# Info and mask spread over the partitions by DMA instead of by matmuls, in a fused convolution, attention and expert kernel

## The chip, the cores and the metric

The kernel runs on one core of a Trainium2 chip (trn2). The metric is the device time of one execution in microseconds, the median of several runs. A core has five engines that run side by side, each through one fixed list of instructions: TensorE (PE) for matmuls, VectorE (DVE), ScalarE (ACT), GpSimd (POOL), and SyncE (SP), which here issues all DMA transfers. They wait for each other through semaphores.

## The reference

The input `x` is 32 images of 64 channels and 32 x 32 pixels. Three layers follow each other, each added to its input:

```python
# layer 1, on the group-normalised input (32 groups of two channels)
info = relu(info_w @ x + info_b)          # 16 rows
mask = sigmoid(mask_w @ x + mask_b)       # 16 rows
expanded = mask[:, :, None] * info[:, None, :]    # 256 rows: each mask row times each info row
x = x + relu(out_w @ expanded + out_b)
# layer 2: linear attention of 8 heads on the layer-normalised tokens, with a two-layer MLP
t = t + attention(layernorm(t))
# layer 3: 8 experts, each W2 @ gelu(W1 @ t + b1) + b2, weighted by the two largest gates
t = t + experts(layernorm(t))
```

What the change touches is `expanded`: each of 16 info rows and 16 mask rows has to stand on the 128 partitions in copies, so that VectorE can multiply them.

## The kernel before

Two images lie on the 128 partitions as a pair, and two pairs ("slots" s = 0 and 1) make a group; there are eight groups. A group goes through some 70 named stages (the *dense* part: statistics, group norm, info and mask, products, `conv_out`, four layer norms, attention, MLP), then the *router* (`gates` to `weights_1`), then 32 expert *units* (expert e, slot s, half c of 512 pixels).

The work of several groups is interleaved. A *turn* runs the dense stages of group a, the router of group a-1 and units of the groups a-1 and a-2. `SCHEDULE` lists the stages of a turn in order; beside each name stand the steps of units that follow it on PE ("H" is a first layer, "Y" a second layer), and how many GELUs on ACT and combines on DVE follow it there. The units before the entry `first_unit` are the last of the older group. All engines run the same list, each with its own part of a stage. Groups 0 and 1 (`EARLY`) are done in an opening of their own (`OPENING`, names with `next` are group 1's), with no units beside them; group 1 uses other buffers there (`convolution_buffers`). Turns 2 to 7 are the full ones.

Info and mask (`info_mask`): PE computes both into PSUM for a slot, 32 rows for each half of the pixels in four strips of 32 partitions; ACT applies ReLU or tanh; DVE splits the result into two float32r parts (`IM`). Six *replicates* a slot (`replicate`, the line of the matmul is L606) copy the rows over the partitions by a matmul with a matrix of zeros and ones, which is loaded at the start (`reps`): for k = 0, 1 first the info rows, which ACT copies to SBUF (`T2`, L921), then the low and the high half of the mask rows, which DVE reads from PSUM and multiplies by info into `BIG` (`product`, L1161, 512 columns at a time). `conv_out` (L617) multiplies `BIG` by the output weights.

PSUM: the dense part has `R[0]` and `R[1]` of two banks each. The units have `HP[0]` and `HP[1]`, of two banks each: unit u computes its first layer into both banks of `HP[u % 2]` (L849), ACT applies GELU over 1024 columns into `H[u % 2]` (L995), the second layer writes its sums into the first bank of the same `HP` (L863), DVE combines them with bias and gate weights into `TM` (`combine`, L1360), and POOL adds them up (`add_up`, L1048). The first layer of unit u therefore waits for the combine of unit u-2.

SP's list: the loads of the start (weights, `reps`, biases, small tables), then turn by turn the gate weights by way of `gates_hbm` into `CWB` (spread over 64 partitions at a time; `gate_rows`, `weights_1`), the next input (`features_1`) and the results (`finish`).

Of the kernel before, what the change touches and what calls it, by code (L numbers as in the profile page):

```python
# [15 lines left out]
P = 128  # L16
# [24 lines left out]
for _name, _width in [  # L41
# [26 lines left out]
    ("channel_stats", "H", 1, 0), ("gates", "Y", 0, 1), ("gate_tokens", "", 0, 1), ("gate_exp", "Y", 1, 0),  # L68
    ("group_stats", "HHY", 1, 0), ("group_norm", "Y", 0, 2), ("choose_1", "", 0, 0), ("info_mask_0", "HHY", 3, 2),
# [17 lines left out]
]  # L87
EARLY = 1
OPENING = [
# [11 lines left out]
    "norm_4.0", "next conv_out.0", "next centre_1.1", "next centre_1.0", "gates", "next rstd_1", "gate_tokens",  # L101
    "gate_exp", "choose_1", "choose_2", "gate_rows", "weights_1", "next norm_1.1", "next norm_1.0",
    "next features_1.0", "next features_1.1",
]
AHEAD = [name.partition(" ")[2] for name in OPENING if name.startswith("next ")]
ROUTER = ("gates", "gate_tokens", "gate_exp", "choose_1", "choose_2", "gate_rows", "weights_1")
FIRST, SECOND = "H", "Y"
BATCH = 2
PE_STEPS, ACT_STEPS, DVE_STEPS = 1, 2, 3
# [17 lines left out]
def build(nc, x, wpack, w1e, reps, out):  # L127
    xd = x.rearrange("(n two) c t -> n (two c) t", two=2)
    od = out.rearrange("(n two) c t -> n (two c) t", two=2)
    with ExitStack() as ctx:  # L130
# [17 lines left out]
        IM = sb("IM", [P, G, 2, CH], F32R)  # L148
# [3 lines left out]
        gates_hbm = nc.dram_tensor("gates_hbm", (G, 2 * E, T), F32).ap()  # L152
        KS = sb("KS", [P, G, NCH, 3, HEADS])
# [4 lines left out]
        SG = sb("SG", [P, 4, G, 1])  # L158
        H = sb("H", [P, 2, 2, CH])
# [15 lines left out]
        REP = sb("REP", [P, NREP, P], F32R)  # L175
# [6 lines left out]
        HP = [psum(f"HP{k}", 2 * CH) for k in range(BATCH)]  # L182
# [15 lines left out]
        raw_reps = BIG[:, 0, 1:3, :].rearrange("p a t -> p (a t)")[:, 0:NREP * P]  # L198
# [39 lines left out]
        r_in = sem("r_in")  # L238
# [9 lines left out]
        gn_stat = sem("gn_stat")  # L248
        gn_dev = sem("gn_dev")
# [5 lines left out]
        hl_high = sem("hl_high")  # L255
        hl_done = sem("hl_done")
        rep_ps = sems("rep_ps")
        ir_done = sems("ir_done")
# [96 lines left out]

        def sums_of(b, u):

            return YR[u % FREE] if last_group(b) else YP[u % BATCH]

# [21 lines left out]
        def turn(a, b, c, par, parts, column):  # L381
# [13 lines left out]
            if a is not None:  # L395
                dense, _ = parts(a, None, par)
                stages.update((name, f) for name, f in dense.items()
                              if (a == 0 or name not in ROUTER) and not name.startswith("finish")
                              and not (a == EARLY and name in AHEAD))
            if a == 0:  # L400
# [51 lines left out]
        def _(sp):  # L452
# [3 lines left out]
            def by_image(t):  # L456
                return t.rearrange("p (k n c) -> p k n c", k=2, c=P)

            rep = by_image(reps[:, 0:NREP * P])
            im_bias = wpack[:, COLS["cols"][0] + B_IM:COLS["cols"][0] + B_IM + 2]  # L460
            for q in range(4):
                there = slice(32 * q, 32 * q + 32)
                sp.dma_start(by_image(raw_reps)[there, :, 0, :], rep[0:32, :, 0, :]).then_inc(r_in, 16)
                sp.dma_start(by_image(raw_reps)[there, :, 1:3, :], rep[32:64, :, 1:3, :]).then_inc(r_in, 16)
# [33 lines left out]
            masks = COLS["headmask"][0]  # L498
            swaps = COLS["ident"][0]
            sp.wait_ge(prep_done, 1)  # L500
            for r, k in crossed(1):
                sp.dma_start(HM2[img(r), P:2 * P], wpack[img(k), masks:masks + P]).then_inc(swap_in, 16)
                sp.dma_start(SWAP[img(r), :], wpack[img(k), swaps:swaps + P]).then_inc(swap_in, 16)

            def parts(a, b, par):
                def next_input(slots):
# [41 lines left out]
                return {**slotwise("features_1", next_input), "gate_rows": gate_weights,  # L548
# [7 lines left out]
        def _(pe):  # L556
# [11 lines left out]
            def parts(a, b, par):  # L568
# [3 lines left out]
                def group_stats():  # L572

                    if a == EARLY:
                        pe.wait_ge(prep_done, 1)
                    for s in range(G):
                        pe.wait_ge(gn_stat, nth(a + 1, s))
                        mm(Ra[s][:, 0:2], w("pairavg"), ST[:, s, 12:14], start=True, stop=True).then_inc(gn_avg, 1)

                def info_mask(s):  # L580


                    pe.wait_ge(gn_done, nth(a + 1, s))
                    for kind in range(2):
# [5 lines left out]
                def replicate(n, slots):  # L590

                    if n == 0 and starting(a):
                        pe.wait_ge(act_prep, 2)
                    for s in slots:
                        if n == 0:
                            pe.wait_ge(hl_done, nth(a + 1, s))
                            if exists(a - 1) and a != EARLY:
# [871 lines left out]
```

## Time and profile before

| | |
|---|---|
| median of 3 runs | 1135.02 us (1130.81 to 1135.02) |
| the profiled execution | 1131.8 us, of which the span from its first to its last instruction is 1129.9 us |
| PE busy | 92% of the span |
| DVE, ACT, POOL busy | 65%, 57%, 36% |
| DMA moved | 88.66 MB |

Busy is the union of an engine's instructions; of matmuls, which overlap, the "mean of one" is longer than the busy time by their number. In a row of the timeline the start, the duration of the merged run, engine, line, operation, destination and sources and the count stand in this order, then in brackets how long the engine waited before it and for whom.

### The profile page before, as it was taken

What the parts mean: (1) busy time and instruction counts of PE and PEld (TensorE: products, weight loads), DVE (VectorE), ACT (ScalarE), POOL (GpSimd) and SP (SyncE); (2) the same over time, 40 slices, a digit from 0 to 9 for tenths busy, and PEclk for the clock granted to TensorE, in tenths of its full rate; (3) what the DMA queues carried; (4) which work ended last, traced back from release to release, by engine and by line L of the source; (5) the groups of instructions that cost most, each with busy time, mean ns of one, the idle gap of its engine ahead of it and who ended that gap; (6) DMA issues with size and microseconds to landing.
All of it is one profiled execution on the core that took longest, in us unless ns stands there. A gap on an engine that the chain in (4) does not pass through costs nothing. (4 is left out here: it accounts for less than half of the span.)

```text
span 1129.9 us, 17149 instructions
## 1 busy us (share of the span) xinstructions
PE 1038.0 (92%) x6678; PEld 445.2 (39%) x6678; DVE 735.4 (65%) x1529; ACT 641.0 (57%) x867; POOL 404.9 (36%) x534
## 2 busy tenths in 40 slices
PE   4888699989999899989999899998999989998997
PEld 2453353324533245323543245332454334532232
DVE  5764744786648866587655966488655886646334
ACT  3354356665665655665656556655566655565554
POOL 0010031352323532344323533235333344224576
PEclk9997889999999999999999999999999999999999
DMA  5000095017700464006710078002760057200860
GB/s 162 6 1 1 1 204 136 21 31 166 164 1 20 97 157 106 1 20 149 160 51 1 19 154 205 1 20 54 157 148 1 19 107 167 50 1 19 198 142 19
DMA packets 15600, 88.66 MB, mean 78 GB/s; under 512 B 3488, under 2 KB 6816, under 8 KB 11424
## 3 DMA queue, kind: packets, MB, share of 16 engines
q1 hardware_dynamic: 15520, 87.57, 33.3%
q8 instruction: 53, 0.87, 0.3%
q14 instruction: 27, 0.22, 0.1%
HBM read 78.12 MB, written 9.44 MB: 77 GB/s over the span
## 5 line engine op out<-in xcount | busy, mean ns | idle before, releaser
L1048 POOL TENSOR_TENSOR XB<-TM,XB 128x256 f32<-128x256 f32 x508 | 366.1, 748 | 570.3 <-DVE TM L1360 570.1
L995 ACT ACTIVATE H<-HP,W 128x1024 f32<-128x1024 f32 x224 | 241.4, 1113 | 182.0 <-PE HP L849 181.7
L1360 DVE SCALAR_TENSOR_TENSOR TM<-HP,B2S,CWB 128x512 f32<-128x512 f32 x224 | 164.9, 747 | 163.7 <-PE HP L863 159.2
L849 PE MATMUL HP<-XF,W1E 64*128 64x512 f32 x1024 | 260.8, 620 | 4.4 <-DVE TM L1360 3.7
L863 PE MATMUL HP<-H,W 128*64 128x512 f32 x896 | 234.3, 613 | 24.2 <-ACT H L995 24.2
L849 PEld LDWEIGHTS HP<-XF,W1E 64*128 64x128 f32 x1024 | 86.2, 186 | 129.5 <-issue 59.7
L863 PEld LDWEIGHTS HP<-H,W 128*64 128x64 f32 x896 | 47.7, 135 | 164.9 <-ACT H L995 111.1
L933 ACT ACTIVATE T<-R 128x512 f32<-128x512 f32 x96 | 57.3, 598 | 45.4 <-PE R L642 38.4
L1161 DVE SCALAR_TENSOR_TENSOR BIG<-R,T 128x512 f32<-128x512 f32 x112 | 70.1, 683 | 14.0 <-PE R L606 13.9
L1248 DVE SCALAR_TENSOR_TENSOR BIG<-T,R 128x512 f32<-128x512 f32 x64 | 41.9, 685 | 38.0 <-ACT T L961 38.0
L606 PE MATMUL R<-IM,REP 32*128 32x512 f32 x336 | 51.3, 470 | 7.7 <-DVE RT L1348 4.4
L1038 POOL TENSOR_TENSOR XB<-XN,X 128x1024 f32<-128x1024 f32 x14 | 33.7, 2410 | 64.6 <-ACT XN L956 64.6
L978 ACT ACTIVATE BIG<-R,BH 128x512 f32<-128x512 f32 x64 | 40.5, 683 | 23.6 <-PE R L790 23.6
L617 PE MATMUL R<-BIG,W 128*64 128x512 f32 x224 | 52.6, 622 | 0.0
L961 ACT ACTIVATE T<-R,MINUS 128x512 f32<-128x512 f32 x64 | 41.4, 688 | 15.7 <-PE R L710 15.0
L1360 DVE SCALAR_TENSOR_TENSOR TM<-R,B2S,CWB 128x512 f32<-128x512 f32 x32 | 24.0, 751 | 38.1 <-PE R L863 35.1
L995 ACT ACTIVATE BIG<-HP,W 128x1024 f32<-128x1024 f32 x32 | 33.9, 1110 | 26.0 <-PE HP L849 26.0
L1223 DVE SCALAR_TENSOR_TENSOR T<-R,T 128x512 f32<-128x512 f32 x64 | 41.0, 683 | 6.8 <-PE R L671 6.8
L606 PEld LDWEIGHTS R<-IM,REP 32*128 32x128 f32 x336 | 24.3, 199 | 50.7 <-DVE BIG L1161 23.4
L921 ACT ACTIVATE T<-R 128x512 f32<-128x512 f32 x56 | 29.8, 599 | 23.3 <-PE R L606 23.3
L1168 DVE TENSOR_TENSOR X<-X,T 128x512 f32<-128x512 f32 x28 | 19.4, 692 | 33.5 <-ACT T L927 33.5
L927 ACT ACTIVATE T<-R,W 128x512 f32<-128x512 f32 x28 | 19.2, 687 | 32.5 <-PE R L617 32.4
(182 smaller groups left out, 1398.8 us busy)
## 6 DMA issues: line engine op xcount, KB each, us to landing
CWB<-gates_hbm SPq DMA_DIRECT2D x32, 1536.0 KB, 20.3
CWB<-gates_hbm SPq DMA_DIRECT2D x32, 512.0 KB, 6.6
out<-XB SPq DMA_DIRECT2D x15, 512.0 KB, 3.1
X<-x SPq DMA_DIRECT2D x14, 512.0 KB, 13.5
XF<-x SPq DMA_DIRECT2D x2, 512.0 KB, 5.9
gates_hbm<-RT SPq DMA_DIRECT2D x16, 64.0 KB, 1.6
W<-wpack SPq DMA_DIRECT2D x1, 968.0 KB, 4.7
W1E<-w1e SPq DMA_DIRECT2D x1, 512.0 KB, 7.2
```

The lines of the kernel that those rows point to most:

```text
L606: last = mm(Ra[s][:, half(c)], REP[rows, n, :], IM[rows, s, part, :], start=(part == 0), stop=(part == 1))
L617: last = mm(Ra[s][img(k), half(c)], w("ow")[:, C * h:C * h + C], BIGa[:, s, 2 * k + h, half(c)], start=(h == 0), stop=(h == 1))
L849: last = mm(HP[u % BATCH][:, half(k)], W1E[img(k), e, :], XF[img(k), 1 - par, s, half(c)], start=True, stop=True)
L863: last = mm(sums_of(b, u)[img(k), :], w("w2e")[:, C * e:C * e + C], activated(b, u)[:, k, :], start=True, stop=True)
L933: f(T2[:, s, half(c)], R[s][:, half(c)], ACT.Square).then_inc(ln_sq[s], 1)
L961: f(T1[:, s, half(c)], R[s][:, half(c)], ACT.Exp, bias=MINUS[:, :]).then_inc(qk_exp[s], 1)
L995: f(activated(b, u).rearrange("p k t -> p (k t)"), HP[u % BATCH][:, :], ACT.Gelu, bias=col(B1E + e))\
L1048: last = nc.gpsimd.tensor_tensor(acc, TM[:, u % BATCH, quarter(0, h)], acc, ALU.add)
L1161: v.scalar_tensor_tensor(out=BIGa[:, s, 2 * k + h, half(c)], in0=Ra[s][:, half(c)], scalar=1.0, in1=T2a[:, s, half(c)], op0=ALU.add, op1=A ...
L1223: return v.scalar_tensor_tensor(out=dst, in0=R[s][:, half(c)], scalar=ROOT_SCALE, in1=T1[:, s, half(c)], op0=ALU.mult, op1=ALU.mult)
L1248: v.scalar_tensor_tensor(out=dst[s][:, half(c)], in0=T1[:, s, half(c)], scalar=1.0, in1=R[s][:, half(c)], op0=ALU.min, op1=ALU.max).then_i ...
L1360: v.scalar_tensor_tensor(out=TM[:, u % BATCH, :], in0=sums_of(b, u), scalar=B2S[:, e % 2, e // 2:e // 2 + 1], in1=CWB[:, s, e, half(c)], o ...
```

## The change

- Info and mask go to a tensor `IMA` in SBUF straight from ACT. The split and the replicates are gone, and so are the load of their matrices, its copy on ACT, and ACT's info copies.
- SP spreads the rows. For each slot it waits for `im_act`, writes the 2 x 32 info rows to `info_hbm`, issues the mask transfers of k = 0 (SBUF to SBUF, for each half h of the mask rows and each half c of the pixels: eight rows, each copied to 16 partitions, 512 columns), waits for the info rows in HBM, reads them back in eight copies into `T2`, and does the same for k = 1 into `XN`. The masks land in `BIG` itself, and the product is formed in place, 1024 columns at a time, from two SBUF operands.
- The stages `channel_stats`, `group_stats`, `group_norm`, `info_mask_0` and `info_mask_1` (`FRONT`) of group a+1 stand in the tail of turn a. For that the group's statistics are copied from PSUM to `GS`, `ROOTS` and `LG` get space of their own, and PE's `spread` of the third and the fourth norm waits until the next group's `GS` copies and `im_act` are done, as they share banks.
- The units' four banks form a ring: `UNIT_BANKS` and `SUM_BANKS` say which two banks unit u % 4 uses for its hidden rows and which one for its sums. For even u the first layer waits for the GELU of unit u-1 instead of the combine of unit u-2, and the GELU waits for the second layer of unit u-2. Unit 3 of four has its banks apart, and its GELU is two instructions of 512 columns. The last group keeps its banks.
- On SP the loads behind `prep_done` become the stage `prepare`. `SCHEDULE` and `OPENING` are new orders of the stages.

The core of the diff:

```diff
+    ("gates", "H", 2, 1), ("gate_tokens", "", 1, 1), ("gate_exp", "YYH", 0, 1), ("choose_1", "HYYH", 3, 2),
+    ("choose_2", "HYHYH", 0, 2), ("low_0.0", "Y", 1, 1), ("gate_rows", "YHHY", 1, 1), ("high_0.0", "", 4, 1),
+    ("low_0.1", "YH", 0, 1), ("high_0.1", "HYYHH", 0, 0), ("low_1.0", "", 0, 2), ("low_1.1", "Y", 0, 0),
+    ("high_1.1", "Y", 0, 0), ("high_1.0", "", 1, 0), ("conv_out.1", "", 0, 1), ("conv_out.0", "", 0, 1),
+    ("centre_1.1", "", 0, 0), ("first_unit", "", 0, 0), ("finish_1", "", 0, 0), ("centre_1.0", "HHY", 1, 0),
...
+    ("hidden_1.1", "Y", 1, 0), ("hidden_out.1", "", 0, 1), ("hidden_out.0", "Y", 0, 1), ("variance_3", "", 0, 0),
+    ("next channel_stats", "", 0, 1), ("rstd_3", "HH", 0, 0), ("next group_stats", "YY", 2, 1),
+    ("spread_3", "", 4, 1), ("norm_3.1", "HHYYHH", 0, 2), ("norm_3.0", "", 0, 0), ("centre_4.1", "Y", 0, 0),
+    ("next group_norm", "Y", 0, 1), ("centre_4.0", "", 0, 0), ("variance_4", "", 0, 0),
+    ("next info_mask_0", "", 0, 0), ("next info_mask_1", "", 1, 1), ("rstd_4", "HH", 2, 0), ("spread_4", "Y", 0, 0),
+    ("norm_4.1", "", 0, 0), ("norm_4.0", "YH", 0, 1),
...
+UNIT_BANKS = [(0, 1), (2, 3), (1, 2), (3, 0)]
+SUM_BANKS = [0, 3, 2, 3]
...
+                def replicate(s):
+
+                    sp.wait_ge(im_act, nth(a + 1, s))
+                    for c in range(NCH):
+                        sp.dma_start(info_hbm[s][:, half(c)], IMa[strip(0, s, c), s, :]).then_inc(info_out[s], 16)
+                    masks(s, 0)
+                    sp.wait_ge(info_out[s], (a + 1) * 16 * NCH)
+                    info(s, 0)
+                    masks(s, 1)
+                    info(s, 1)
+
+                def info(s, k):
+
+                    sp.dma_start(INFO[k][:, s, :], info_hbm[s, IC * k:IC * k + IC, :].unsqueeze(0).broadcast_to([P // IC, IC, T]))\
+                        .then_inc(info_in[k][s], 16)
+
+                def masks(s, k):
+
+                    for h in range(2):
+                        for c in range(NCH):
+                            row = strip(1, s, c).start + IC * k + HD * h
+                            sp.dma_start(BIGa[:, s, 2 * k + h, half(c)],
+                                         IMa[row:row + HD, s, :].unsqueeze(1).broadcast_to([HD, P // HD, CH]))\
+                                .then_inc(mask_in[k][h][s], 16)
+
+                INFO = (T2a, XNa)
...
+                    if EARLY < a + 1 < GROUPS:
+                        if k == 3:
+                            pe.wait_ge(gn_copied, nth(a + 2, G - 1))
+                        if k == 4:
+                            pe.wait_ge(im_act, nth(a + 2, G - 1))
...
+                    elif u % 2 == 0 and (u > 0 or exists(b - 1)):
+                        pe.wait_ge(gelu_done, b * US + u)
                     elif u >= BATCH or exists(b - 1):
                         pe.wait_ge(comb_done, b * US + u + 1 - BATCH)
...
-                    for s, c in pieces(slots):
-                        if h == 0:
-                            dve.wait_ge(ir_done[s], at(a * 2 + k + 1, c))
-                        dve.wait_ge(rep_ps[s], at(a * NREP + 3 * k + h + 2, c))
-                        v.scalar_tensor_tensor(out=BIGa[:, s, 2 * k + h, half(c)], in0=Ra[s][:, half(c)], scalar=1.0,
-                                               in1=T2a[:, s, half(c)], op0=ALU.add, op1=ALU.mult)\
+                    for s in slots:
+                        dve.wait_ge(info_in[k][s], (a + 1) * 16)
+                        dve.wait_ge(mask_in[k][h][s], (a + 1) * 16 * NCH)
+                        v.scalar_tensor_tensor(out=BIGa[:, s, 2 * k + h, :], in0=BIGa[:, s, 2 * k + h, :], scalar=1.0,
+                                               in1=(T2a, XNa)[k][:, s, :], op0=ALU.add, op1=ALU.mult)\
                             .then_inc(prod_done[s], 1)
```

In the new `OPENING` the products of group 0 stand in the order `low_0.0`, `high_0.0`, `low_1.0`, `low_0.1`, `high_0.1`, `high_1.0`, `low_1.1`, `high_1.1`, group 1's info and mask after `rstd_1`, and its last product `next high_1.1` between `variance_4` and `rstd_4`.

## Rows read from the trace of the kernel before

**Rows 1.** The page: busy time by engine, and the DMA queue that SP feeds.

```profile
PE 1038.0 (92%) x6678; PEld 445.2 (39%) x6678; DVE 735.4 (65%) x1529; ACT 641.0 (57%) x867; POOL 404.9 (36%) x534
...
q1 hardware_dynamic: 15520, 87.57, 33.3%
```

**Rows 2.** Groups by line and shape: count, busy us, mean ns, idle before.

```profile
L1048 POOL TENSOR_TENSOR XB<-TM,XB 128x256 f32<-128x256 f32 x508 | 366.1, 748 | 570.3 <-DVE TM L1360 570.1
...
L849 PE MATMUL HP<-XF,W1E 64*128 64x512 f32 x1024 | 260.8, 620 | 4.4 <-DVE TM L1360 3.7 <-ACT BIG L995 0.3
L995 ACT ACTIVATE H<-HP,W 128x1024 f32<-128x1024 f32 x224 | 241.4, 1113 | 182.0 <-PE HP L849 181.7
L863 PE MATMUL HP<-H,W 128*64 128x512 f32 x896 | 234.3, 613 | 24.2 <-ACT H L995 24.2
...
L1161 DVE SCALAR_TENSOR_TENSOR BIG<-R,T 128x512 f32<-128x512 f32 x112 | 70.1, 683 | 14.0 <-PE R L606 13.9
...
L606 PE MATMUL R<-IM,REP 32*128 32x512 f32 x336 | 51.3, 470 | 7.7 <-DVE RT L1348 4.4 <-DVE IM L1153 1.6 <-ACT T L921 1.5
...
L978 ACT ACTIVATE BIG<-R,BH 128x512 f32<-128x512 f32 x64 | 40.5, 683 | 23.6 <-PE R L790 23.6
```

**Rows 3.** The timeline of PE over the six full turns.

```profile
223.60 1.07 PE L817 MATMUL R<-XF,GWZ 128*32 128x256 f32 x16 [0.72 <-DVE XF L1223]
...
490.92 1.07 PE L817 MATMUL R<-XF,GWZ 128*32 128x256 f32 x16 [0.72 <-DVE XF L1223]
...
515.41 0.85 PE L606 MATMUL R<-IM,REP 32*128 32x512 f32 x8 [0.73 <-DVE RT L1348]
...
530.36 0.75 PE L606 MATMUL R<-IM,REP 32*128 32x512 f32 x8
...
532.95 7.09 PE L617 MATMUL R<-BIG,W 128*64 128x512 f32 x32
...
616.38 1.08 PE L658 MATMUL R<-T,LINES 128*32 128x128 f32 x32
...
619.73 1.08 PE L863 MATMUL HP<-H,W 128*64 128x512 f32 x4 [0.20 <-ACT H L995]
...
1025.49 1.07 PE L817 MATMUL R<-XF,GWZ 128*32 128x256 f32 x16 [0.72 <-DVE XF L1223]
```

**Rows 4.** Windows: each engine's busy time, then granted clock, DMA share, GB/s.

```profile
80.00:84.00 4.00, 1.78 (x38) 1.14 (x36) 3.62 (x11) 2.56 (x6) 0.00 (x0) 1.00 0.00 0
88.00:92.00 4.00, 4.00 (x10) 1.46 (x10) 2.27 (x4) 1.26 (x2) 0.00 (x0) 0.50 0.00 0
14.00:16.00 2.00, 1.42 (x8) 0.00 (x0) 0.77 (x2) 1.64 (x3) 0.00 (x0) 1.00 1.04 426
533.00:535.00 2.00, 2.00 (x12) 0.72 (x12) 0.70 (x2) 0.39 (x2) 0.49 (x1) 1.00 0.97 197
```

**Rows 5.** DMA issues: KB each, median us from issue to landing.

```profile
gates_hbm<-RT SPq DMA_DIRECT2D x16, 64.0 KB, 1.6
```

**Rows 6.** The timeline of all engines in the opening.

```profile
2.12 0.43 SPq L463 DMA_DIRECT2D BIG<-reps  x1
...
5.41 0.43 SPq L464 DMA_DIRECT2D BIG<-reps  x1
...
27.59 5.81 SPq L497 DMA_DIRECT2D GB<-wpack  x16
...
41.29 3.65 PE L617 MATMUL R<-BIG,W 128*64 128x512 f32 x16
...
47.55 1.92 PE L586 MATMUL HP<-CWB,W 128*32 128x512 f32 x16
```

**Rows 7.** The timeline of VectorE in the opening.

```profile
55.21 2.73 DVE L1153 TENSOR_TENSOR IM<-CWB,IM 128x512 fp32r<-128x512 f32 x1
...
114.94 1.29 DVE L1161 SCALAR_TENSOR_TENSOR CWB<-HP,CWB 128x512 f32<-128x512 f32 x2 [1.20 <-PE HP L606]
```

**Rows 8.** The timeline of GpSimd in the opening.

```profile
54.79 5.38 POOL L1038 TENSOR_TENSOR XB<-XN,X 128x1024 f32<-128x1024 f32 x2 [53.14 <-ACT XN L956]
```

More of the change, by code:

```diff
@@ L89 @@
 OPENING = [
[11 rows of a table removed]
-    "norm_4.0", "next conv_out.0", "next centre_1.1", "next centre_1.0", "gates", "next rstd_1", "gate_tokens",
-    "gate_exp", "choose_1", "choose_2", "gate_rows", "weights_1", "next norm_1.1", "next norm_1.0",
-    "next features_1.0", "next features_1.1",
+    "channel_stats", "group_stats", "group_norm", "info_mask_0", "info_mask_1", "low_0.0", "high_0.0",
+    "next channel_stats", "low_1.0", "low_0.1", "high_0.1", "prepare", "high_1.0", "next group_stats",
[11 rows of a table added]
 ]
 AHEAD = [name.partition(" ")[2] for name in OPENING if name.startswith("next ")]
+FRONT = ("channel_stats", "group_stats", "group_norm", "info_mask_0", "info_mask_1")
 ROUTER = ("gates", "gate_tokens", "gate_exp", "choose_1", "choose_2", "gate_rows", "weights_1")
@@ L152, in build @@
         gates_hbm = nc.dram_tensor("gates_hbm", (G, 2 * E, T), F32).ap()
+        info_hbm = nc.dram_tensor("info_hbm", (G, 2 * IC, T), F32).ap()
         KS = sb("KS", [P, G, NCH, 3, HEADS])
@@ L158, in build @@
         SG = sb("SG", [P, 4, G, 1])
+        GS = sb("GS", [P, G, 2])
+        IMA = sb("IMA", [P, G, CH])
+        ROOTS = sb("ROOTS", [P, 4, P])
+        LG = sb("LG", [P, T // 4])
         H = sb("H", [P, 2, 2, CH])
@@ L181, in build @@
         R = [psum(f"R{s}", T) for s in range(G)]
-        HP = [psum(f"HP{k}", 2 * CH) for k in range(BATCH)]
+        HB = psum("HB", 2 * BATCH * CH)
+        HP = [HB[:, 2 * CH * k:2 * CH * (k + 1)] for k in range(BATCH)]
         FREE = 2 * BATCH
@@ L254, in build @@
         im_act = sem("im_act")
[L255 to L258, printed above, removed]
+        info_out = sems("info_out")
+        info_in = [sems(f"info_in{k}_") for k in range(2)]
+        mask_in = [[sems(f"mask_in{k}{h}_") for h in range(2)] for k in range(2)]
         prod_done = sems("prod_done")
@@ L354, in last_group, with hidden_banks, bank @@
             return b == GROUPS - 1
+        def hidden_banks(b, u):
+            if last_group(b):
+                return 2 * (u % BATCH), 2 * (u % BATCH) + 1
+            return UNIT_BANKS[u % FREE]
+        def bank(k):
+            return HB[:, CH * k:CH * (k + 1)]
         def sums_of(b, u):
-            return YR[u % FREE] if last_group(b) else YP[u % BATCH]
+            return YR[u % FREE] if last_group(b) else bank(SUM_BANKS[u % FREE])
         def activated(b, u):
@@ L397, in turn @@
                 stages.update((name, f) for name, f in dense.items()
-                              if (a == 0 or name not in ROUTER) and not name.startswith("finish")
+                              if (a == 0 or name not in ROUTER + FRONT) and not name.startswith("finish")
                               and not (a == EARLY and name in AHEAD))
+                if 0 < a < GROUPS - 1:
+                    following, _ = parts(a + 1, None, 1 - par)
+                    stages.update((f"next {name}", following.get(name)) for name in FRONT)
             if a == 0:
@@ L436, in convolution_buffers, with info_and_mask @@
             return X, XN, T1, T2, BIG, R
+        def info_and_mask(a):
+            return CWB[:, :, 1, 0:CH] if a == EARLY else IMA
         def gate_banks(a):
@@ L497, in _, with prepare @@
                 sp.dma_start(GB[E * i:E * i + E, :], gb).then_inc(gb_in, 16)
[L498 to L503, printed above, removed]
-            def parts(a, b, par):
+            def prepare():
+                masks = COLS["headmask"][0]
+                swaps = COLS["ident"][0]
+                sp.wait_ge(prep_done, 1)
+                for r, k in crossed(1):
+                    sp.dma_start(HM2[img(r), P:2 * P], wpack[img(k), masks:masks + P]).then_inc(swap_in, 16)
+                    sp.dma_start(SWAP[img(r), :], wpack[img(k), swaps:swaps + P]).then_inc(swap_in, 16)
+            def parts(a, b, par):
+                XNa, _, T2a, BIGa = convolution_buffers(a)[1:5]
+                IMa = info_and_mask(a)
+                def replicate(s):
[18 more added lines that the diff above has]
+                INFO = (T2a, XNa)
                 def next_input(slots):
@@ L583, in info_mask @@
                     pe.wait_ge(gn_done, nth(a + 1, s))
+                    if a > EARLY:
+                        pe.wait_ge(cp_done, a * (LNS - 1) * len(PIECES))
                     for kind in range(2):
@@ L588, in info_mask @@
                     last.then_inc(im_ps, 1)
[L590 to L597, printed above, removed]
-                                pe.wait_ge(cwt_done, a)
-                        elif n % 3 == 1:
-                            pe.wait_ge(ir_done[s], at(a * 2 + n // 3 + 1, LAST))
-                        else:
-                            pe.wait_ge(prod_done[s], at(a * 4 + (n + 1) // 3 + n // 3, LAST))
-                        for part in range(2):
-                            for c in range(NCH):
-                                rows = strip(1 if n % 3 else 0, s, c)
-                                last = mm(Ra[s][:, half(c)], REP[rows, n, :], IM[rows, s, part, :], start=(part == 0), stop=(part == 1))
-                                if part == 1:
-                                    last.then_inc(rep_ps[s], 1)
                 def conv_out(slots):
@@ L612, in conv_out @@
                         pe.wait_ge(prep_done, 1)
+                    if exists(a - 1) and a != EARLY:
+                        pe.wait_ge(cwt_done, a)
                     for s, c in pieces(slots):
-                        pe.wait_ge(prod_done[s], at(a * 4 + 4, c))
+                        pe.wait_ge(prod_done[s], a * 4 + 4)
                         for h in range(2):
@@ L848, in first_layer @@
                     for k in range(2):
-                        last = mm(HP[u % BATCH][:, half(k)], W1E[img(k), e, :], XF[img(k), 1 - par, s, half(c)],
+                        last = mm(bank(hidden_banks(b, u)[k]), W1E[img(k), e, :], XF[img(k), 1 - par, s, half(c)],
                                   start=True, stop=True)
@@ L914, in info_mask @@
                     info, mask = img(s), img(1 - s)
-                    f(T1a[info, s, 0:CH], Ra[s][info, 0:CH], ACT.Relu, bias=BI[info, 0, 0:1])
-                    f(T1a[mask, s, 0:CH], Ra[s][mask, 0:CH], ACT.Tanh, bias=BT[mask, :], scale=0.5).then_inc(im_act, 1)
-                def info(k, slots):
-                    for s, c in pieces(slots):
-                        act.wait_ge(rep_ps[s], at(a * NREP + 3 * k + 1, c))
-                        f(T2a[:, s, half(c)], Ra[s][:, half(c)], ACT.Copy).then_inc(ir_done[s], 1)
+                    f(IMa[info, s, :], Ra[s][info, 0:CH], ACT.Relu, bias=BI[info, 0, 0:1])
+                    f(IMa[mask, s, :], Ra[s][mask, 0:CH], ACT.Tanh, bias=BT[mask, :], scale=0.5).then_inc(im_act, 1)
                 def conv_out(slots):
@@ L994, in gelu @@
                         act.wait_ge(y_ps, b * US + u + 1 - FREE)
-                    f(activated(b, u).rearrange("p k t -> p (k t)"), HP[u % BATCH][:, :], ACT.Gelu, bias=col(B1E + e))\
-                        .then_inc(gelu_done, 1)
+                    if not last_group(b) and u % 2 == 0 and (u > 0 or exists(b - 1)):
+                        act.wait_ge(y_ps, b * US + u + 1 - BATCH)
+                    low, high = hidden_banks(b, u)
+                    if high > low:
+                        f(activated(b, u).rearrange("p k t -> p (k t)"), HB[:, CH * low:CH * high + CH], ACT.Gelu, bias=col(B1E + e))\
+                            .then_inc(gelu_done, 1)
+                        return
+                    f(activated(b, u)[:, 0, :], bank(low), ACT.Gelu, bias=col(B1E + e))
+                    f(activated(b, u)[:, 1, :], bank(high), ACT.Gelu, bias=col(B1E + e)).then_inc(gelu_done, 1)
                 def expert(step, u):
@@ L1003, in parts @@
                     "info_mask_0": lambda: info_mask(0), "info_mask_1": lambda: info_mask(1),
-                    **slotwise("info_0", lambda slots: info(0, slots)), **slotwise("info_1", lambda slots: info(1, slots)),
                     **slotwise("conv_out", conv_out), **slotwise("centre_1", lambda slots: square(1, slots)),
@@ L1128, in group_stats @@
                         dve.wait_ge(gn_avg, nth(a + 1, s))
+                        v.tensor_copy(GS[:, s, :], Ra[s][:, 0:2]).then_inc(gn_copied, 1)
+                    for s in range(G):
+                        dve.wait_ge(gn_copied, nth(a + 1, s))
                         dve.wait_ge(gn_stat, nth(a + 1, s))
-                        v.tensor_tensor(ST[:, s, 14:15], ST[:, s, 12:13], Ra[s][:, 0:1], ALU.subtract)\
+                        v.tensor_tensor(ST[:, s, 14:15], ST[:, s, 12:13], GS[:, s, 0:1], ALU.subtract)\
                             .then_inc(gn_dev, 1)
```

41 lines of the change are left out of this document (9 added, 32 removed), and 47 rows, old and new, of tables (OPENING, SCHEDULE).

## The prediction

> **What bounds the kernel now.** I read the busy table first: TensorE (PE) is busy 92% of a 1129.9 us span, no other engine over 65%, and the DMA queue that SP feeds uses 33.3% of its sixteen engines [rows 1]. The groups by line say what PE does: the experts' two matmul lines take most, the replicate matmuls of L606 51.3 us [rows 2]. Then the timeline of PE. The turns are regular: the gates' matmul of six turns runs from 223.60 to 1025.49 us, 133.65 us a turn. In the turn that starts at 490.92, the replicates run from 515.41, the convolution's output from 532.95 to 540, the fourth variance from 616.38 [rows 3]. PE waits about 6.6 us in that turn (14 gaps, of which the rows show 0.72, 0.73 and 0.20). So PE is the bound, and a gap anywhere in its order goes to the end: each engine runs one fixed order, and nothing overtakes a waiting instruction.
>
> **What leaves.** A group's 48 replicate matmuls: in that turn the timeline shows them in seven runs of 0.73 to 1.33 us, 6.5 us with overlaps, 6.1 without (the first and the last run stand in [rows 3]). ScalarE loses its info copies (it is 57% busy), VectorE its two splits a slot (65%), all beside PE [rows 1]. The products stay: sixteen halves of 0.63 us busy a group (70.1/112) [rows 2] become eight of 1024 columns, by the same row some 1.25 each, with both inputs in SBUF.
>
> **What the ring of four gives.** First layers wait for VectorE's combine 4.4 us in the whole span, second layers for ScalarE 24.2 [rows 2]. The ring takes away half of the first and some of the second: 0 to 2 us a turn, I take 1. Its price is a GELU cut in two for every fourth unit, 2 x 0.68 for 1.11 (the 512 and the 1024-column rows [rows 2]), 0.25 us on an engine with room.
>
> **What comes: the transfers.** For each slot SP writes the info rows to HBM (two issues), then eight mask transfers of 256 KB (8 SBUF rows, each copied 16 times) and two info transfers of 512 KB. A group of two slots moves 4.19 MB of masks and 2.10 MB of info. All wait on `im_act` in a turn's tail, and all products wait on them. No row before has an SBUF source, so the rate has to be bounded.
>
> The two end rows: the loads into 128 partitions move 426 GB/s; the gate weights, spread over 64 partitions at a time, move 197 GB/s where nothing else runs, with the engines' share at 0.97 [rows 4]. So half of the partitions give half of the rate while the engines look fully busy: the rate follows the partitions touched. Fast end: the gate weights' 197, a broadcast on the same queue. Slow end: in proportion, 197 x 8/64 = 24.6 for eight source rows. Sixteen engines at 426 are 26.6 each, one such share per eight partitions; eight rows use between one and eight shares. I take two, 53 GB/s: close to the slow end, since both measured rates lie on the proportional line. Info reads HBM and writes all partitions; I give it eight shares, 213.
>
> The Trainium skill (SBUF — State Buffer, "Door 1: the DMA port swizzle") says that four neighbouring partitions and the four 32 further share one of sixteen ports. Eight mask rows from a multiple of eight then lie on two ports, both column halves of a mask on the same two; strict proportion from the rows would make the sum below about 2260 us, the page's ports about 1530. The 64-partition row agrees with it; no row here shows a read.
>
> Let D be the time of a group's transfers. At 53.2: a mask is 262,144 B / 53.2 = 4.93 us, sixteen are 78.9, four infos of 2.46 are 9.8, so D = 88.7. SP needs only some 24 issues of 0.43 us [rows 6] and isn't the limit.
>
> **A turn.** From `im_act` of slot 0 to the first mask: two issues and a landing like that of the gates' rows (1.6 us [rows 5]), 2.6. After the last landing, two products, 2.5. From the convolution's output to the end of the fourth variance 84.5 (616.38 + 1.08 - 532.95 [rows 3]); to that, one more expert step that now stands there (four matmuls of 0.255, 1.02 [rows 2]), the group statistics and a slot's info and mask matmuls (some 1.5; 0.96 of it half of the run at 47.55 [rows 6]) and two 512-column activations (1.36 [rows 2]): 3.9. A turn becomes D + 93.5, if that is longer than PE's work, 133.65 - 6.1 - 1 = 126.5. At D = 88.7 it is 182.2, that is 48.6 more; six turns, 292. The gates' weights queue behind the masks (SP's issues are in order) but are wanted later than conv_out: nothing. Stores and next inputs come when the queue is empty.
>
> Who stands behind the wait: VectorE at `low_0.1`, and behind it its combines, so PE's expert units stop two or three steps later. The work put ahead of the products is some 32 expert steps of 1.02, 33 us, and the router: it covers a D of some 33 us, not 89.
>
> **The opening.** No units exist there, so group 0's transfers lie bare. SP reaches them only after its list of loads: that ended at 27.59 + 5.81 = 33.4 us, less the eight loads of `reps` that go, from 2.12 to 5.84: 29.6 [rows 6]. Group 0's second conv_out started at 41.29 [rows 6]; it now starts at 29.6 + 2.6 + D + 2.5 = 123.4, 82 later. Group 1's info and mask (matmuls from 47.55, `im_act` some three us later) shift as much, to 133; its transfers and products end at 133 + 5.1 + 88.7 = 227, while the product that needed them stood at 114.94, now 197 [rows 6, 7]: 30 more. Less some 4 us of replicates in that chain, the opening costs 108.
>
> **Sum.** Against the profiled execution's own time, 1131.8 us (1.9 over its span; the median is 1135.0, 0.3% higher): 1131.8 + 292 + 108 = 1532, call it 1530 us. Left out: PE's granted clock after long gaps. In the opening, after PE had waited more than half of 80 to 84 us, the clock stood at 0.50 (the level of 1.2 GHz) from 88 to 92 [rows 4]; a gap of 37 us a turn may cost some 3 us each, up to 18.
>
> **Rivals.**
> *The transfers hide* (the other side: faster). If eight source rows feed the queue as fast as the gate weights flow, D = 6.29 MB / 197 = 31.9. The turn is PE's 126.5, 7.1 less, six times 43. The opening loses (D + 34.7) - 41.3 - 4 = 21. Time 1110. The decision lies at D = 36: turn 129.5, 25 gained, 25 lost in the opening, so masks of about 160 GB/s. For it: the lead in the tail fits D of 32. Against it: the halved rate at 64 partitions.
> *A middle rate.* Four shares, 106 GB/s: D = 39.4 + 9.8 = 49.2, a turn 142.7, 9 x 6 = 54; the opening 39 or so (group 1's products no longer wait). Time 1225.
> *Products against GpSimd* (the change brings nothing though transfers hide). Where VectorE had both inputs in SBUF, a 512-column `IM` subtraction (a product's half is 0.63 [rows 2]) took 2.73 us while GpSimd's adds from 54.79 ran [rows 7, 8]. GpSimd's adds (0.75 each [rows 2]) now run beside the products; eight products, each held by one, are 6 us a turn on VectorE, 36 in six. On top of the hidden case: 1146. In my forecast VectorE waits there anyway, and it costs nothing. The Trainium skill (SBUF — State Buffer, "Who interferes with whom") says that a VectorE instruction with two SBUF inputs and a GpSimd instruction that reads SBUF exclude each other; by it alone the saving of the replicates would be gone, and the one row agrees.
>
> **Chances and range.** Slow transfers near 53 GB/s (1350 to 1600): 0.45. A middle rate or a hidden transfer with held products, over 0.5% slower: 0.22. Hidden and faster: 0.27. Within 0.5%, about what this kernel's measurement can tell from no change: 0.06. Slower is 0.67 in all. The likeliest case's own range is 1350 to 1600. Cases of both signs hold much of the chance, so the range reaches from 1095 (hidden, two us a turn more from the ring) to 1580 (with the clock's 18 and some more); proportional transfers beyond 1580 and the lowest corner are left out, some 15 in 100.
>
> **What would show it.** In the DMA issues, `BIG<-IMA` of 256 KB landing a multiple of 5 us after issue, those late in a slot over 30, and the GB/s of that stretch near 50 to 60 with few engines' shares filled. In the waits, VectorE's products behind DMA `BIG<-IMA` or `T2<-info_hbm` for 30 to 40 us in each of six turns, PE's combine and conv_out waits behind them, and gates some 182 us apart. The first conv_out matmul of the second slot near 123 us. L606 gone, ScalarE and VectorE busy time down a little. Wrong if masks land within 3 us of each other's issue at 150 GB/s or more: then PE stays over 90% busy, the gates are 126 to 128 us apart, and only the opening is longer.

## The result, and the profile after

The changed kernel takes 1509.47 us (median of 4 runs, 1504.29 to 1512.05), the kernel before 1135.02 (1130.81 to 1135.25): ratio 1.331, 95% interval 1.328 to 1.335. The profiled execution's span is 1502.5 us against 1129.9. Two executions of masks by way of HBM and one of the eight in 2 KB pieces, of four each, fell in a slower state of the chip and are left out of the times below.

The page of the changed kernel: busy time by engine, the queue, the chain that ended last.

```profile
PE 1030.5 (69%) x6294; PEld 424.4 (28%) x6294; DVE 714.4 (48%) x1449; ACT 616.5 (41%) x858; POOL 424.5 (28%) x534
...
q1 hardware_dynamic: 38176, 139.61, 45.0%
...
PE 43%; SPq 37%; DMA 8%; DVE 5%; ACT 4%; issue 3%; POOL 0%; DVEq 0%; POOLq 0%
SPq L542 24%; PE HB L885 8%; PE HB L899 7%; SPq L534 6%; DMA XN<-info_hbm 6%; SPq L525 5%; PE R L646 4%; PE R L671 4%; PE R L735 2%; PE R L822 2%; PE R L824 2%; ACT H L1026 2%; PE R L831 2%; PE R L899 2%; PE R L753 2%
```

PE has 384 matmuls fewer and is busy 7.5 us less than in [rows 1], but that is now 69% of a longer span. A quarter of the chain is the mask transfers' issues (L542): four of them take SP 10.48 us below, against 0.43 for one in [rows 6], presumably because its queue is full, which no row shows. The timeline of PE shows where (the gates' matmul is now L851, `conv_out` L646, first layers L885):

```profile
239.04 1.07 PE L851 MATMUL HB<-XF,GWZ 128*32 128x256 f32 x16
339.72 1.07 PE L851 MATMUL R<-XF,GWZ 128*32 128x256 f32 x16
...
516.79 1.07 PE L851 MATMUL R<-XF,GWZ 128*32 128x256 f32 x16
...
580.06 2.08 PE L885 MATMUL HB<-XF,W1E 64*128 64x512 f32 x4 [32.21 <-DVE TM L1387]
...
597.43 9.00 PE L646 MATMUL R<-BIG,W 128*64 128x512 f32 x32 [7.85 <-DVE BIG L1188]
...
694.98 1.07 PE L851 MATMUL R<-XF,GWZ 128*32 128x256 f32 x16
...
1402.53 1.07 PE L851 MATMUL R<-XF,GWZ 128*32 128x256 f32 x16
```

Before, the first gates stood here, in the same view of the kernel before:

```profile
128.03 1.07 PE L817 MATMUL HP<-XF,GWZ 128*32 128x256 f32 x16
```

With [rows 3] the 372.6 us are found whole. The opening to the first gates: 239.04 - 128.03 = 111.0. From there to the next gates, a stretch whose tail now holds group 2's front: 100.7 against 95.6, 5.1. The six full turns: 1062.8 against 801.9, that is 177.1 a turn against 133.65, 260.9. After the last gates: 100.0 against 104.4, 4.4 less.

In a turn PE stops for long twice, 32.21 us at a first layer, behind a combine, and 7.85 at `conv_out`. The waits, summed over the span, name what VectorE stood at (total, times, longest):

```profile
DVE BIG L1188 <- DMA T<-info_hbm: 290.3, 14, 43.4
...
PE HB L885 <- DVE TM L1387: 229.1, 26, 33.8
```

and SP's own timeline in that turn, what was under way:

```profile
511.37 0.79 SPq L525 DMA_DIRECT2D info_hbm<-IMA  x2
512.20 10.48 SPq L542 DMA_DIRECT2D BIG<-IMA  x4
522.73 4.28 SPq L534 DMA_DIRECT2D T<-info_hbm  x1
527.04 11.03 SPq L542 DMA_DIRECT2D BIG<-IMA  x4
...
581.60 2.78 SPq L534 DMA_DIRECT2D XN<-info_hbm  x1
```

From the first issue at 511.37 to `conv_out` at 597.43 are 86.0 us. The windows (columns as in [rows 4]) give the rate, for masks in the first two and for info in the third:

```profile
515.00:517.00 2.00, 2.00 (x12) 0.46 (x12) 2.00 (x4) 0.09 (x1) 0.00 (x0) 1.00 0.48 49
519.00:521.00 2.00, 2.00 (x10) 0.51 (x10) 1.40 (x5) 1.26 (x2) 1.01 (x2) 1.00 0.47 48
535.00:537.00 2.00, 2.00 (x10) 0.70 (x10) 0.00 (x0) 0.40 (x1) 0.25 (x1) 1.00 0.50 197
```

At 48 and at 197 GB/s the share is the same, half of the sixteen engines. So two things could hold the masks back: what each engine gets out of the source, and how many engines work.

### The profile page after: what moved, and what is told of

Same layout as the page of the kernel before. It is cut to its first block, busy times and chain, and to the rows that moved or that the text cites. A ratio compares the mean times of both kernels' runs of the same rounds, so it can differ in the third digit from the quotient of the medians.

```text
span 1502.5 us, 16595 instructions
## 1 busy us (share of the span) xinstructions
PE 1030.5 (69%) x6294; PEld 424.4 (28%) x6294; DVE 714.4 (48%) x1449; ACT 616.5 (41%) x858; POOL 424.5 (28%) x534
## 4 chain that ended last, share of the span: by engine, by line
PE 43%; SPq 37%; DMA 8%; DVE 5%; ACT 4%; issue 3%; POOL 0%; DVEq 0%; POOLq 0%
SPq L542 24%; PE HB L885 8%; PE HB L899 7%; SPq L534 6%; DMA XN<-info_hbm 6%; SPq L525 5%; PE R L646 4%; PE R L671 4%; PE R L735 2%; PE R L822 2%; PE R L824 2%; ACT H L1026 2%; PE R L831 2%; PE R L899 2%; PE R L753 2%
## 5 line engine op out<-in xcount | busy, mean ns | idle before, releaser
L885 PE MATMUL HB<-XF,W1E 64*128 64x512 f32 x1024 | 280.7, 646 | 230.1 <-DVE TM L1387 229.1
L1026 ACT ACTIVATE H<-HB,W 128x1024 f32<-128x1024 f32 x168 | 184.6, 1113 | 426.0 <-PE HB L885 425.9
L899 PE MATMUL HB<-H,W 128*64 128x512 f32 x896 | 248.5, 650 | 19.3 <-ACT H L1026 18.2
L1387 DVE SCALAR_TENSOR_TENSOR TM<-HB,B2S,CWB 128x512 f32<-128x512 f32 x224 | 164.2, 745 | 144.9 <-PE HB L899 132.5
L885 PEld LDWEIGHTS HB<-XF,W1E 64*128 64x128 f32 x1024 | 83.5, 190 | 395.1 <-DVE TM L1387 278.9
L1188 DVE SCALAR_TENSOR_TENSOR BIG<-BIG,T 128x1024 f32<-128x1024 f32 x28 | 36.3, 1301 | 290.3 <-DMA T<-info_hbm 290.3
L646 PE MATMUL R<-BIG,W 128*64 128x512 f32 x224 | 66.1, 754 | 53.1 <-DVE BIG L1188 53.1
L899 PEld LDWEIGHTS HB<-H,W 128*64 128x64 f32 x896 | 49.6, 140 | 176.7 <-ACT H L1026 79.3
L1188 DVE SCALAR_TENSOR_TENSOR BIG<-BIG,XN 128x1024 f32<-128x1024 f32 x28 | 36.3, 1333 | 74.1 <-DMA XN<-info_hbm 74.1
L1029 ACT ACTIVATE H<-HB,W 128x512 f32<-128x512 f32 x56 | 38.3, 683 | 26.9 <-PE HB L885 26.5
L646 PEld LDWEIGHTS R<-BIG,W 128*64 128x64 f32 x224 | 21.3, 175 | 97.1 <-issue 97.1
L1026 ACT ACTIVATE BIG<-HB,W 128x1024 f32<-128x1024 f32 x32 | 33.9, 1111 | 25.9 <-PE HB L885 25.9
```

The source lines that it names most:

```text
L646: last = mm(Ra[s][img(k), half(c)], w("ow")[:, C * h:C * h + C], BIGa[:, s, 2 * k + h, half(c)], start=(h == 0), stop=(h == 1))
L885: last = mm(bank(hidden_banks(b, u)[k]), W1E[img(k), e, :], XF[img(k), 1 - par, s, half(c)], start=True, stop=True)
L899: last = mm(sums_of(b, u)[img(k), :], w("w2e")[:, C * e:C * e + C], activated(b, u)[:, k, :], start=True, stop=True)
L1026: f(activated(b, u).rearrange("p k t -> p (k t)"), HB[:, CH * low:CH * high + CH], ACT.Gelu, bias=col(B1E + e))\
L1188: v.scalar_tensor_tensor(out=BIGa[:, s, 2 * k + h, :], in0=BIGa[:, s, 2 * k + h, :], scalar=1.0, in1=(T2a, XNa)[k][:, s, :], op0=ALU.add, ...
L1387: v.scalar_tensor_tensor(out=TM[:, u % BATCH, :], in0=sums_of(b, u), scalar=B2S[:, e % 2, e // 2:e // 2 + 1], in1=CWB[:, s, e, half(c)], o ...
```

## The experiments

Each ratio is against the kernel before, run on the same chip, with its 95% interval. Theory A: the eight neighbouring partitions that a transfer reads set the mask rate.

**Mask rows two and four partitions apart.** The columns of the mask weights and biases are reordered, so that the eight rows of a transfer lie 2 or 4 partitions apart; bytes, transfers and order stay. With 4:

```diff
-    row = strip(1, s, c).start + IC * k + HD * h
-    IMa[row:row + HD, s, :]
+    row = strip(1, s, c).start + 2 * k + h
+    IMa[row:row + 4 * HD - 3:4, s, :]
```

> The mask rows of one transfer lie two partitions apart (16 partitions spanned instead of 8), by another order of the mask weights' columns and biases on the host; bytes, descriptors, issues and engines are the same. Theory A (the rate follows the paths that the eight source rows lie on): in the changed kernel 86.0 us pass from im_act to conv_out, of which 80.9 are transfers, 4.4 a mask; twice the paths halve the masks to 35.5 + 9.8, the turn falls from 178.2 to some 143, and the time to about 1235 us. Rival B (small pieces, few engines, or SP's issue set the rate, whatever the source): no change, 1500 to 1515. Rival C (a read from SBUF is slow as such): no change either.

> The mask rows of one transfer lie four partitions apart, over 32 partitions; otherwise as before. Theory A: the masks of a group fall to about 18 us, all transfers to 28, the wait before conv_out goes, a turn is PE's 126 to 130 us, and the time 1110 to 1135 us. Rivals B and C: 1500 to 1515.

Measured: 1263.73 us with 2 (a single execution, so no interval), and with 4 1217.53, ratio 1.076 (1.073 to 1.080). The order of A holds, nothing else was moved: 1509, 1264, 1218. With 2 the masks of slot 0 go at twice the rate, at the same share of the engines:

```profile
434.00:436.00 2.00, 2.00 (x22) 0.71 (x20) 1.65 (x3) 1.25 (x2) 0.93 (x2) 1.00 0.50 97
```

A turn takes some 145 us, near A's 143, though the whole time is missed by 29. With 4 the rate doesn't double again, and A's hidden case is missed by over 80 us. Windows and SP's timeline with 4:

```profile
424.00:428.00 4.00, 2.98 (x14) 0.80 (x12) 3.70 (x7) 3.96 (x6) 3.14 (x4) 1.00 0.53 135
428.00:432.00 4.00, 2.97 (x14) 0.70 (x12) 3.83 (x11) 1.77 (x3) 0.83 (x2) 1.00 0.54 136
```

```profile
419.19 2.50 SPq L525 DMA_DIRECT2D info_hbm<-IMA  x2
421.73 7.76 SPq L542 DMA_DIRECT2D BIG<-IMA  x4
437.60 0.57 SPq L534 DMA_DIRECT2D T<-info_hbm  x1
```

The rate is nearly three times that of the neighbouring rows, and the share is still half. In the second view SP is done issuing slot 1's masks at 429.49 and then waits 8 us for slot 1's info rows, whose small store queues behind slot 0's transfers.

**Masks by way of HBM.** The mask rows are stored beside the info rows and read back from HBM, in the same transfers:

```diff
-    IMa[row:row + HD, s, :]
+    info_hbm[s, row:row + HD, half(c)]
```

> The mask rows go to HBM with the info rows and are read back from there, in the same 256 KB transfers of 2 KB pieces from eight rows. Theory A: the source's partitions no longer matter, a group's transfers take some 30 us plus 2 for the way there, 1110 to 1140 us. Rival B: 1500 to 1530, as pieces, engines and issues are the same. Rival C: as A.

Measured: 1208.46 and 1222.11 us, ratio 1.072 (1.067 to 1.078), outside every range that was said. No source partition is left, and the time is that of rows 4 apart. The windows: 181 to 206 GB/s while the transfers flow, and a dry stretch while slot 1's store is awaited.

```profile
436.00:440.00 4.00, 2.92 (x14) 0.72 (x12) 3.73 (x9) 3.15 (x4) 2.18 (x3) 1.00 0.53 200
...
444.00:446.00 2.00, 2.00 (x12) 0.64 (x10) 1.20 (x4) 0.60 (x1) 2.00 (x4) 1.00 0.08 29
```

**Stores of both slots first.** With rows 4 apart, the info rows of both slots are stored ahead of all mask transfers.

> As the run with mask rows four partitions apart, but SP issues both slots' info rows to HBM before the bulk of the transfers. In that run SP waits 8 to 16 us for slot 1's info rows, which queue behind slot 0's masks, and the queue runs dry meanwhile. Theory D (that wait is part of what was left): the transfers flow at 138 GB/s (masks) and 197 (info) without a break, 41 us a group, the turn falls from 142 to some 136 to 138, the time from 1217 to 1170 to 1190. Rival (the bytes alone set it): 1210 to 1220.

Measured: 1215.7 us, 1.071 (1.064 to 1.079), as without it and as the rival said: with the 8 us wait gone nothing is gained. What is left is the bytes at this rate.

**Eight copies or sixteen outermost.** Both kernels take masks and info from HBM, store both slots first, and move each mask in one transfer of 512 KB (pieces of 4 KB). They differ in the outermost dimension of the transfers: eight as before, or sixteen (16 copies of the 8 mask rows; 16 info rows of 8 copies), with the rows of `out_w` reordered to match. Which of rows and copies is outermost turns over with it, for masks and info alike, and no run moved that alone:

```diff
-    info_hbm[s, row:row + HD, :].unsqueeze(1).broadcast_to([HD, P // HD, T])
+    info_hbm[s, row:row + HD, :].unsqueeze(0).broadcast_to([P // HD, HD, T])
```

> Masks and info by way of HBM, both slots' rows stored first, and a mask transfer covers both halves (512 KB in 4 KB pieces, still eight rows outermost). Theory E (eight of sixteen engines work: the share is 0.50 at 197 GB/s): 31 us a group plus 3 for the stores, turn 129 to 132, 1135 to 1155. Rival (2 KB pieces were what held the masks at 140 to 170): nearer 1120.

> As the run before, but with sixteen copies or sixteen rows outermost in each transfer (the rows of the output weights are reordered on the host for it). Theory E: all sixteen engines work, 300 GB/s or more, 20 us a group, the transfers hide, a turn is PE's 126 to 128, the time 1100 to 1115, faster than the kernel before by 2 to 3%. Rival (something else than the number of engines holds the spread at 200 GB/s): 1135 to 1155, as the eight-engine run.

Measured: 1270.22 us, 1.124 (1.118 to 1.130), with eight, and 1128.51, 0.996 (0.994 to 0.997), with sixteen. The theory's direction holds and both sizes miss. With eight the windows show little more than half of what sixteen give (232 to 238 GB/s, windows below):

```profile
448.00:452.00 4.00, 3.10 (x14) 0.76 (x12) 3.52 (x7) 3.96 (x5) 2.91 (x4) 1.00 0.53 130
```

**The same eight with 2 KB pieces**, since eight outermost came out slower than masks by way of HBM had been:

> As hbm8_first (both slots' rows stored to HBM first, then all transfers back to back, eight rows outermost), but each mask transfer again covers one half of the pixels: 256 KB in pieces of 2 KB instead of 512 KB in pieces of 4 KB. Theory P, the longer pieces with eight rows outermost slowed hbm8_first: the transfers go at 143 to 202 GB/s as in masks_hbm without its dry stretch, so 1190 to 1225 us (ratio 1.05 to 1.08), 45 to 80 below hbm8_first. Rival O, the order slowed it, since transfers that follow each other back to back get in each other's way: 1255 to 1285 us, as hbm8_first, at 115 to 135 GB/s.

Measured: 1177.48 to 1188.08 us, ratio 1.049 (1.043 to 1.055), the times a little under P's range. The order of the transfers isn't what slowed them; their size or that of their pieces is, which were halved together. The same part of the turn:

```profile
412.00:416.00 4.00, 2.90 (x12) 0.80 (x12) 3.76 (x9) 3.42 (x4) 2.44 (x4) 1.00 0.51 181
...
424.00:428.00 4.00, 3.35 (x14) 0.70 (x12) 0.91 (x2) 1.76 (x4) 2.84 (x4) 1.00 0.55 198
```

Why the longer ones are slower stays open. Pieces of 4 KB as such aren't slow with eight outermost: info, read in such pieces, went at 197 (the window from 535 above), but there the copies are outermost and not the rows. And sixteen with pieces of 4 KB may not escape it: 236 GB/s over sixteen engines is 14.8 each, 130 over eight 16.3, and 181 over eight in pieces of 2 KB 22.6. No run had sixteen with pieces of 2 KB.

**Small tables after the first transfers.** In the kernel with sixteen, SP reaches group 0's stores at 29.26 us, after its list of small tables (44 issues from 7.96, 17.37 and on); here they stand behind group 0's transfers (of the four loops, `GB`'s is shown).

```diff
-            for i in range(P // E):
-                sp.dma_start(GB[E * i:E * i + E, :], gb).then_inc(gb_in, 16)
             def prepare():
+                for i in range(P // E):
+                    sp.dma_start(GB[E * i:E * i + E, :], gb).then_inc(gb_in, 16)
```

> As the sixteen-engine run, with the small tables' loads (some 40 issues of SP) put behind group 0's info and mask transfers in the opening, where SP reached those transfers only at 29.3 us. Theory: 10 to 13 us less than the sixteen-engine run, all of it in the opening. Rival (group 0's chain has other slack, or the tables are late now): no difference or slower.

Measured: 1115.61 us, 0.984 (0.982 to 0.986): 1.6% faster than the kernel before, the interval well below 1, and 12.9 us below the kernel with sixteen, as the theory said. Its windows and its gates:

```profile
498.00:502.00 4.00, 4.00 (x30) 1.31 (x30) 2.20 (x7) 2.77 (x4) 2.79 (x4) 1.00 0.83 192
502.00:506.00 4.00, 3.78 (x16) 0.80 (x12) 3.58 (x6) 2.12 (x2) 3.19 (x4) 1.00 1.04 232
506.00:510.00 4.00, 3.19 (x14) 0.80 (x12) 3.52 (x7) 3.95 (x4) 2.83 (x4) 1.00 1.03 237
```

```profile
138.49 1.07 PE L856 MATMUL HB<-XF,GWZ 128*32 128x256 f32 x16
...
498.12 1.07 PE L856 MATMUL R<-XF,GWZ 128*32 128x256 f32 x16
...
511.36 1.13 PE L890 MATMUL HB<-XF,W1E 64*128 64x512 f32 x4
...
627.77 1.07 PE L856 MATMUL R<-XF,GWZ 128*32 128x256 f32 x16
```

The engines' share is 1.03. The opening still loses 10.5 us (138.49 against 128.03); with the tables ahead it was 24.5, with the first gates here:

```profile
152.50 1.07 PE L856 MATMUL HB<-XF,GWZ 128*32 128x256 f32 x16
```

A turn is 129.65 with either, against 133.65.

**The ring of four.** Alone on the kernel before, taken out of the changed kernel, and taken out of the fastest one. Out means:

```diff
-UNIT_BANKS = [(0, 1), (2, 3), (1, 2), (3, 0)]
-SUM_BANKS = [0, 3, 2, 3]
+UNIT_BANKS = [(0, 1), (2, 3), (0, 1), (2, 3)]
+SUM_BANKS = [0, 2, 0, 2]
...
-                    elif u % 2 == 0 and (u > 0 or exists(b - 1)):
-                        pe.wait_ge(gelu_done, b * US + u)
```

> The kernel before with the units' banks as a ring of four, nothing else, in its old order of stages. By the prediction's step 0 to 2 us a full turn, 1 taken: 1123 to 1135 us, about 1129. Rival: the GELU cut in two and the new waits cost more than the combine's wait gives: 1136 to 1150.

> The changed kernel with the ring of four taken out: units use their two bank pairs in turn, and each first layer waits for the combine of the unit before the last. Theory C, what the ring rides out (a combine held for some 5 us behind the router's chain on VectorE) happens here while the masks are still on their way, so a wait ahead of them is covered: 1500 to 1530 us, ratio 1.325 to 1.35. Rival, the units ahead of the first product get less far without the ring and that work is done after the products, as in hbm16_noring: 10 us a turn more, 1560 to 1590 us, ratio 1.375 to 1.40.

> hbm16_tables with the ring of four taken out again: units use their two bank pairs in turn, and each first layer waits for the combine of the unit before the last. Theory N, the ring is worth nothing here either (as in ring_only): 1112 to 1119 us, ratio 0.981 to 0.987 against the kernel before. Rival, it pays in the new order, where first layers wait 15.3 us for combines in the whole span even with the ring (4.4 in the kernel before): doubled to 30, 1125 to 1135 us. A gain from the ring's removal (the split GELU gone, first layers at 618 ns again instead of 632) would show as 1100 to 1110 us.

Measured: alone, 1136.16 us, 1.001 (1.000 to 1.003), worth nothing. Out of the changed kernel, 1538.03, 1.355 (1.352 to 1.359): some 29 us worse, between the two theories and in the range of neither. The stretch from the first gates to the next, which waits for no masks, takes 9.5 us more there (110.2 against 100.7), a full turn 2.8. Out of the fastest, 1188.15, 1.048 (1.046 to 1.050), 72 us worse, far outside what either theory said. There VectorE, PE and the windows show it, in the same place of the turn as the rows above (gates at 527.24):

```profile
536.23 0.75 DVE L1390 SCALAR_TENSOR_TENSOR TM<-HB,B2S,CWB 128x512 f32<-128x512 f32 x1 [0.15 <-PE HB L902]
536.90 0.41 DVE L1333 TENSOR_REDUCE RT<-RT 128x32 f32<-128x256 f32 x1
...
541.42 0.68 DVE L1368 TENSOR_TENSOR RT<-RT 128x64 f32<-128x64 f32 x4
541.97 0.74 DVE L1390 SCALAR_TENSOR_TENSOR TM<-HB,B2S,CWB 128x512 f32<-128x512 f32 x1
```

```profile
539.18 1.08 PE L902 MATMUL HB<-H,W 128*64 128x512 f32 x4 [1.01 <-ACT H L1029]
542.77 2.08 PE L888 MATMUL HB<-XF,W1E 64*128 64x512 f32 x4 [2.51 <-DVE TM L1390]
```

```profile
541.00:543.00 2.00, 0.23 (x2) 0.23 (x4) 1.65 (x7) 0.00 (x0) 0.21 (x1) 0.78 1.04 238
543.00:545.00 2.00, 2.00 (x6) 0.50 (x8) 0.00 (x0) 0.10 (x1) 1.19 (x2) 0.50 1.01 229
...
553.00:555.00 2.00, 2.00 (x10) 0.60 (x8) 1.54 (x2) 0.56 (x1) 1.73 (x3) 1.00 0.37 92
```

From 536.90 VectorE does 5 us of the router (`choose_2`) in one piece, and the combine behind it starts at 541.97. With the ring the combines stand behind the same piece (from 507.92 there):

```profile
512.99 1.40 DVE L1392 SCALAR_TENSOR_TENSOR TM<-HB,B2S,CWB 128x512 f32<-128x512 f32 x2
```

Without the ring the first layer waits for that combine, 2.51 us. In the window of that gap PE is busy 0.23 of 2 us, and the granted clock goes to 0.50, the level of 1.2 GHz, until the window from 551 (0.66); the four matmuls that took 1.13 us take 2.08. With the ring the same first layer asks only for the GELU of the unit before (511.36 above, no wait). A turn is 139.7 us in place of 129.65: by PE's groups 7.0 more of waiting at first layers, 0.2 at second, 3.0 more busy.

## Why the prediction was right, step by step

Forecast 1530 us, measured 1509, in the likeliest case and by its mechanism; the sizes of the terms, in turn:

- **The mask rate.** Two shares, 53 GB/s, were said; 48 and 49 are measured with slot 0. The rows bounded it only between one share and eight, and two was a choice among them; the strides bear it out (97 from rows 2 apart). Info at eight shares, 213, was measured at 197.
- **A turn.** 182.2 was said, 177.1 measured, by two errors that partly cancel. From slot 0's first store to `conv_out` 93.8 (D + 5.1) was said and 86.0 measured in the turn shown, 7.8 too much. Of the 2.6 us before the first mask 1.6 were a landing that masks from SBUF don't wait for: they were issued 0.83 us behind the first store (512.20 against 511.37). And D took 82.7 (from there to 594.93, the end of VectorE's last wait for a transfer) where 88.7 was said, though masks at 48.5 GB/s throughout would have made it some 97: behind slot 0's first info the queue went faster (windows of 48 to 101 GB/s from 539 to 575), perhaps as masks and info ran side by side, which no run shows. The rest, 93.5 - 5.1 = 88.4, measured 178.2 - 86.0 = 92.2, 3.8 more. Of that 1.9 is `conv_out`, 9.00 us against 7.09 in [rows 3], with the granted clock at 0.50 from 595 to 599 and at 0.71 to 603: the slow clock after the gaps, left out of the sum and put at some 3. Where the other 1.9 went isn't shown.
- **The turns' sum.** 292 was said for six; 260.9 is measured, plus 5.1 for the stretch before them and less 4.4 at the end.
- **The opening.** 108 was said, 111.0 measured, in part by luck: the terms miss both ways. SP's list ended at 29.25 (29.6 was said), but group 0's second `conv_out` started at 115.39, not 123.4, and group 1's first store at 127.57, not 133. VectorE's last wait for group 1's transfers ended at 210.79, where the sum has some 224 (227 less two products). The last product still started only at 226.23, without waiting for a transfer: it stands behind `variance_4` in VectorE's order, a term that the sum doesn't have.
- **Who stands behind the wait.** VectorE at `low_0.1`, the combines behind it, PE's first layers: the row of 32.21 us.
- **The ring.** 0 to 2 us a turn, 1 taken. Alone it is worth nothing. In the new order it is worth far more, since there the combine waits behind the router, which the rows of before, with only 4.4 us of such waits [rows 2], couldn't show. In the changed kernel most of that is covered by the transfers: 2.8 us a turn against 9.4 in the fastest one (means of six), while the stretch that waits for no masks loses much the same in both (9.5 and 10.2).
- **The hidden case, said 1110.** The kernel in which the transfers hide takes 1128.5, and 1115.6 with the tables moved too. Its turn is 129.65 where 126.5 was said. PE's busy time fell by 4.2 (126.98 to 122.81 from gates to gates), not 6.1: the replicates went, but first layers took 35.1 against 32.5. The other 1 us is the one credited to the ring. The decision was put at masks of about 160 GB/s; eight outermost in 2 KB pieces, at 181 to 198, still ended at 1.049, with a turn of 135.9 (402.24 to 538.14), so it lay higher.
- **Products against GpSimd.** 6 us a turn was the bound. The groups of VectorE in one turn of the fastest kernel, where the products meet GpSimd's adds:

```profile
L1193 DVE SCALAR_TENSOR_TENSOR BIG<-BIG,XN 128x1024 f32<-128x1024 f32 x4 | 6.3, 1622 | 0.0
L1193 DVE SCALAR_TENSOR_TENSOR BIG<-BIG,T 128x1024 f32<-128x1024 f32 x4 | 5.6, 1394 | 0.0
```

  11.9 us for eight, against 10 at the estimated 1.25: some 2 us.

What the prediction didn't separate is a second limit. It read half a rate as half of the partitions; here half of the engines is a limit of its own, which stands when the source partitions are out of the way (share 0.51 to 0.56 with eight outermost, 1.03 with sixteen). The Trainium skill (DMA: Bandwidth & Descriptors, "Why a DMA increments its semaphore by 16 and not by 1") says that the slowest dimension of a transfer that isn't 1 sets how many engines take part; these shares agree. That a share of 1.03 isn't yet full speed shows too: the spread moved 232 to 238 GB/s at it, the loads at the start 426 at 1.04 [rows 4]. What holds it there wasn't tried.

## What to carry to other kernels

Before a broadcast moves from matmuls to DMA, read in the windows the share and the GB/s together: a share of 0.5 with low GB/s was two limits here, few engines and a slow source, and each needed its own cure (sixteen outermost; rows apart or by way of HBM). A wait that is worth nothing in one order of the work can be worth 10 us a turn in another, so a part of a change is to be tried in the order it was made for. Where a group's transfers now stand at the head of the chain, what SP issues ahead of them is paid for in full: without the tables SP got there at 15.26 in place of 29.26, and the first gates came 14.0 us earlier.

## What the hardware showed unexpectedly

- SBUF sources: masks at 48 to 49 GB/s from eight neighbouring partitions, 95 to 98 with the same rows 2 apart; with rows 4 apart masks and info together at 119 to 156, and from HBM at 181 to 206, each at about half of the engines.
- With eight rows outermost, masks in pieces of 4 KB (info among them) went at 116 to 140 GB/s, in pieces of 2 KB at 163 to 203, at nearly the same share; with sixteen, pieces of 4 KB went at 232 to 238, per engine no faster than with eight. No cause was shown.
- Behind one gap of 2.51 us on PE, with one of 1.01 shortly ahead of it, the granted clock stood at 0.50 from 543 to 551 us, at 1.00 from 553. With the ring, stops of 1.02 and 0.94 us in the same place left it at 1.00.
